# A graph network's edge loop: rings and body of eight groups, loads split evenly over two queues, and the table P in three bf16 parts

## The chip, the cores and the metric

The kernel is one program on one core of a Trainium2 chip. The metric is the device time of the program in microseconds (us); lower is better. The engines are TensorE (PE, with its weight loads as PEld), VectorE (DVE), ScalarE (ACT), GpSimd (POOL) and SyncE (SP). SP, ACT and POOL also issue DMA transfers.

## The reference

Four graph networks run one after the other on 3,125 nodes and 103,125 edges, each followed by a residual and a layer norm. The change touches the second, called L1: node features are 128 wide, and four layers update them along the edges.

```python
for i in range(L):                                      # L = 4
    ef = jnp.concatenate([h[row], h[col], edge_attr], axis=1)
    ef = jax.nn.silu(ef @ edge_w1[i] + edge_b1[i])
    ef = jax.nn.silu(ef @ edge_w2[i] + edge_b2[i])
    ef = ef * edge_mask
    agg = jax.ops.segment_sum(ef, row, num_segments=n)
    nf = jnp.concatenate([h, agg], axis=1)
    nf = jax.nn.silu(nf @ node_w1[i] + node_b1[i])
    nf = nf @ node_w2[i] + node_b2[i]
    h = (h + nf) * node_mask
```

## The kernel before

**Tables.** The first edge product is split: P = h @ W1[0:128] and Q = h @ W1[128:256] are worked out once per node and layer and stored in DRAM as p_tab and q_tab, in 25 blocks of 128 nodes. For each block PE does one product of 256 columns (line 1715), DVE copies it out of PSUM (line 1724), and SP writes its halves (lines 1730, 1731) from two buffers.

**The edge loop.** The edges, sorted on the chip, fill 840 tiles of 128, three tiles to a group, so 280 groups in each layer (`edge_mlp`). For a group:

- `first` (PE) sums into the PSUM area z1, 128 features by 384 edges: the edge attributes (line 1515), for each of the three tiles a block of P times a one-hot matrix that picks each edge's row (line 1517), for the third tile of three groups in four a block of Q picked in the same way (line 1519), and for the other tiles rows of Q that POOL gathered by an indirect DMA (issue at line 1472), turned by a transpose (line 1522);
- `one` (ACT, line 1574) is the first Silu, from z1 to h1;
- `second` (PE, line 1531) multiplies h1 by W2 into z2, which holds the bias beforehand; `two` (ACT, line 1581) is the second Silu, from z2 to h2; `seed` (DVE, line 1607) then puts the bias into z2 for the next group;
- `sums` (PE, line 1542) adds h2 through a weighted one-hot matrix into the PSUM columns of the target nodes. Their addresses are loaded into PE's registers once for two groups (line 963, called from `sums`).

DVE builds the one-hots: `oht` for P (line 1618), `ohn` for Q (line 1617), `ohm` for the sums (line 1626), and hands POOL the indices (line 1602).

**Order.** Every engine works its own program, with semaphores between them. PE's step for group n is first(n), sums(n-2), second(n-1). ACT's is two(n-2), one(n), and for even n its fetch. There is one z1 and one z2, so first(n) waits for one(n-1), and sums(n) and second(n+1) wait for seed(n), which waits for two(n).

**Transfers.** All inputs of a group lie in rings of four slots. For a pair of groups SP issues the row numbers for `oht` (`places`) and `ohn` (`nears`), the edge attributes (`eat`), one or two blocks of Q, and four blocks of P (lines 1495, 1496). ACT issues the other two blocks of P (line 1567), in its own program between one(n) and two(n-1). SP and ACT load the DRAM addresses into registers before (line 963). The pair n, n+1 is fetched once z1 of group n-3 is done.

**The loop.** `turns` writes out two rounds of four groups, then a hardware loop (branch at line 932) whose body is four groups, run 67 times, then a last round.

Of the kernel before, what the change touches and what calls it, by code (L numbers as in the profile page):

```python
# [13 lines left out]
P = 128  # L14
# [6 lines left out]
U = 4  # L21
# [4 lines left out]
M3 = 3  # L26
G3 = NT // M3
K3 = G3 // U
GW = M3 * P
NONE = U - 1  # L30
NA = K3 * NONE
# [23 lines left out]
def gnn_kernel(nc, a, out):  # L55

    with ExitStack() as ctx:
# [51 lines left out]
        p_tab = dram("p_tab", [NP, HID])  # L109
# [817 lines left out]
        def turns(eng, step, rounds=K):  # L927

            for k in (0, 1):
                for h in range(U):  # L930
                    step(k, h)
            with eng.Fori(2, rounds - 1) as k:
                for h in range(U):
                    step(k, h)
            for h in range(U):
                step(rounds - 1, h)
# [494 lines left out]
        m_got = [sem(f"m_got{h}") for h in range(U)]  # L1431
        m_pl, m_sp, m_act = ([sem(f"m_{n}{q}") for q in range(2)] for n in ("pl", "sp", "act"))
        Z1, Z2 = 3584, NP

        def edge_mlp(layer, we36, w2, b1, b2):
# [4 lines left out]
            def here(k, h, lag=0):  # L1440
                return there(k, h, lag, G3)

            def gathered(h):
                return 3 if h == NONE else 2

            with ExitStack() as st:
                qidx = sb(f"qidx{layer}", [P, U, M3], I32, st)
                qg = sb(f"qg{layer}", [P, U, M3, HID], F32, st)
                pb = sb(f"pb{layer}", [P, U, M3, HID], F32, st)
                qb = sb(f"qb{layer}", [P, U, HID], F32, st)  # L1450
                places = sb(f"places{layer}", [P, U, GW], BF16, st)
                nears = sb(f"nears{layer}", [P, U, P], BF16, st)
                eat = sb(f"eat{layer}", [36, U, GW], BF16, st)
                oht = sb(f"oht{layer}", [P, U, GW], F32, st)
                ohn = sb(f"ohn{layer}", [P, U, P], F32, st)
# [5 lines left out]
                with nc.Block() as block:  # L1461
                    @block.gpsimd
                    def _(pool):
                        def gather(k, h):
                            n = k * U + h
                            if here(k, h, U):

                                pool.wait_ge(m_z1, g0 + n - U + 1)
# [5 lines left out]
                        turns(pool, gather, K3)  # L1474

                    @block.sync
                    def _(sp):
                        def fetch(k, h):
                            if h % 2:
                                return  # L1480
                            q, n = h // 2, k * U + h
                            if here(k, h, U):
# [9 lines left out]
                            for i in range(2 - q):  # L1492
# [5 lines left out]
                        turns(sp, fetch, K3)  # L1498

                    @block.tensor  # L1500
                    def _(pe):
# [5 lines left out]
                        def first(k, h):  # L1507

                            n, q = k * U + h, h // 2
                            if here(k, h, 1):  # L1510
                                pe.wait_ge(m_h1, g0 + n)
                            pe.wait_ge(m_sp[q], 16 * (7 - q) * (k0 + k + 1))
                            pe.wait_ge(m_act[q], 32 * (k0 + k + 1))
# [4 lines left out]
                            if h != NONE:  # L1518
# [6 lines left out]
                        def second(k, h):  # L1525

                            n = k * U + h
# [6 lines left out]
                        def sums(k, h):  # L1534

                            n = k * U + h
                            if h % 2 == 0:
                                to[:] = address(mybir.EngineType.PE, to_p[0:1, bass.ds(k * 2 + h // 2, 1), :].rearrange("a g j -> a (g j)"), (NB - 1) * P)
# [6 lines left out]

                        def step(k, h):
                            first(k, h)
# [4 lines left out]
                        turns(pe, step, K3)  # L1552
                        sums(K3 - 1, U - 2)
                        second(K3 - 1, U - 1)
                        sums(K3 - 1, U - 1)

                    @block.scalar
                    def _(act):
                        def fetch(k, h):
                            q, n = h // 2, k * U + h  # L1560
                            if not here(k, h):
                                return
                            if here(k, h, U):
                                act.wait_ge(m_z1, g0 + n - 2)
                            at = address(mybir.EngineType.Activation, at_p[0:1, bass.ds(n + 1, 1), 1:3].rearrange("a g j -> a (g j)"), (NB - 1) * P)
                            for j in range(2):
                                act.dma_start(pb[:, h + 1, 1 + j, :], p_tab[bass.ds(at[j], P), :]).then_inc(m_act[q], 16)

                        def one(k, h):
                            n = k * U + h  # L1570
# [5 lines left out]
                        def two(k, h):  # L1576
                            n = k * U + h
# [5 lines left out]
                        def step(k, h):  # L1583
# [3 lines left out]
                            if h % 2 == 0:  # L1587
                                fetch(*moved(k, h, 2))
                        fetch(0, 0)
                        turns(act, step, K3)  # L1590
                        two(K3 - 1, U - 2)
                        two(K3 - 1, U - 1)

                    @block.vector
                    def _(dve):
                        def indices(k, h):
                            if not here(k, h):
                                return
                            if here(k, h, U):
# [353 lines left out]
```

## Time and profile before

| | |
|---|---|
| median of 3 runs | 8,981.45 us (8,978.94 to 8,988.67) |
| the profiled execution | 9,007.83 us, its span 9,006.1 us |
| mean granted clock of TensorE | 0.792 |
| L1's edge loops, four of them | within 2,367.5 to 6,366 us |
| PE, DVE, ACT, POOL busy | 74%, 56%, 31%, 57% of the span |

The median of the runs is the figure that the change is compared with. The profile comes from another, single execution, somewhat longer than the median, and every duration in the text is from it. Times in the views are counted from the start of its span. A matmul of f32 operands appears as two instructions in the trace, one of bf16 as one.

### The profile page before, as it was taken

To read this page: it belongs to the slowest core of one execution; us is meant where nothing else is said; L and a number is where in the kernel's file an instruction comes from. 1 tells how busy PE (TensorE), PEld (TensorE's weight loads), DVE (VectorE), ACT (ScalarE), POOL (GpSimd) and SP (SyncE) were. 2 spreads that over 40 slices of the span, in tenths; PEclk is the share of its full clock that TensorE was granted. 3 is DMA by queue.
4 is the path that set the end of the run, shared out by engine and by line. 5 is a ranking of instruction groups with operands and counts; after the bars stand their busy time and mean duration, and the time that the engine had idled before them with its cause. 6 is when DMAs were issued, how large, how long until landed. Compare 5 with 4: busy or idle time off the path is not lost. (4 is left out here: it accounts for less than half of the span.)

```text
span 9006.1 us, 230609 instructions
## 1 busy us (share of the span) xinstructions
PE 6678.6 (74%) x51782; PEld 5543.5 (62%) x51783; DVE 5014.9 (56%) x13561; ACT 2799.6 (31%) x8299; POOL 5100.8 (57%) x7138
## 2 busy tenths in 40 slices
PE   1222226767799978999799988999766666888998
PEld 1111114555577757777577767878455555786998
DVE  6333346867355545555455545555322222998999
ACT  1222204544233323333233322333133333222554
POOL 3777736755366636666366645666167776221554
PEclk8555555555799989999899999999655555998999
DMA  2000004433366646666455555666311000332232
GB/s 63 3 3 3 3 29 138 119 100 110 110 166 165 164 112 165 165 166 164 107 164 164 164 121 159 169 166 167 90 31 7 7 7 6 78 82 57 73 72 60
DMA packets 1288626, 877.60 MB, mean 97 GB/s; under 512 B 448518, under 2 KB 1192859, under 8 KB 1287640
## 3 DMA queue, kind: packets, MB, share of 16 engines
q1 hardware_dynamic: 991510, 618.55, 25.3%
q0 software_dynamic: 134272, 178.98, 9.3%
q10 hardware_dynamic: 162752, 78.98, 3.1%
q8 instruction: 41, 0.67, 0.0%
q14 instruction: 51, 0.42, 0.0%
HBM read 832.60 MB, written 50.91 MB: 98 GB/s over the span
## 5 line engine op out<-in xcount | busy, mean ns | idle before, releaser
L1472 POOL DMA_INDIRECT qg<-q_tab,qidx x2520 | 2393.5, 950 | 1444.0 <-DVE qidx L1602 736.5
L1607 DVE COPY ps<-b 128x384 f32<-128x384 f32 x1120 | 628.2, 561 | 1640.7 <-ACT h L1581 1609.1
L1067 PE MATMUL ps<-rhs_i,ohi 128*128 128x128 f32 (+2 forms) x8640 | 1215.1, 266 | 209.8 <-issue 198.0
L1067 PEld LDWEIGHTS ps<-rhs_i,ohi 128*128 128x128 f32 (+1 forms) x8640 | 998.8, 162 | 340.3 <-issue 281.2
L1033 POOL COPY near<-x 128x48 bf16 x2160 | 675.7, 351 | 788.4 <-PE ps L1056 432.9
L1542 PE MATMUL ps<-ohm,h 128*128 128x128 f32 x6720 | 1001.1, 285 | 146.6 <-DVE ps L1607 136.6
L1195 POOL DMA_INDIRECT got_m<-y_tab,idx_m x832 | 815.5, 980 | 474.2 <-issue 251.7
L1517 PE MATMUL ps<-oht,pb 128*128 128x128 f32 x6720 | 1060.5, 295 | 0.0
L1574 ACT ACTIVATE h<-ps,b 128x384 f32<-128x384 f32 x1120 | 650.2, 581 | 1292.6 <-PE ps L1522 1245.2
L1542 PEld LDWEIGHTS ps<-ohm,h 128*128 128x128 f32 x6720 | 842.0, 192 | 281.5 <-issue 275.7
L1581 ACT ACTIVATE h<-ps 128x384 f32<-128x384 f32 x1120 | 549.1, 490 | 1432.5 <-PE ps L1531 1343.5
L375 POOL DMA_INDIRECT list_by_src<-ring,rpos x808 | 783.0, 969 | 348.7 <-issue 255.0
L1212 PE MATMUL ps<-rhs_m,ohi_m 128*128 x2880 | 668.4, 403 | 415.5 <-ACT rhs_m L1238 386.7
L1517 PEld LDWEIGHTS ps<-oht,pb 128*128 128x128 f32 x6720 | 845.2, 193 | 196.9 <-issue 196.9
L1626 DVE TENSOR_SCALAR ohm<-iota_row,loc_p,w_p 128x128 f32<-128x128 f32 x3360 | 961.0, 347 | 0.0
L1531 PE MATMUL ps<-w,h 128*128 128x128 f32 x6720 | 940.2, 276 | 0.0
L1128 DVE TENSOR_TENSOR ohi<-iota_row,dst_i 128x512 f32<-128x512 f32 (+1 forms) x1080 | 929.9, 861 | 0.0
L1212 PEld LDWEIGHTS ps<-rhs_m,ohi_m 128*128 128x128 f32 x2880 | 636.7, 328 | 448.0 <-issue 447.8
L1531 PEld LDWEIGHTS ps<-w,h 128*128 128x128 f32 x6720 | 847.6, 193 | 0.0
L1252 DVE TENSOR_TENSOR ohi_m<-iota_row,dst_i 128x512 f32<-128x512 f32 x360 | 249.2, 693 | 833.5 <-PE ps L1212 829.4
L1123 DVE TENSOR_SCALAR oht_i<-places_i,iota_p 128x512 bf16<-128x512 bf16 (+1 forms) x1080 | 512.5, 475 | 177.6 <-PE ps L1067 160.1
L1031 POOL COPY near<-z 128x384 bf16 x720 | 344.8, 508 | 375.9 <-PE ps L1056 305.0
(438 smaller groups left out, 8629.8 us busy)
## 6 DMA issues: line engine op xcount, KB each, us to landing
pb<-p_tab SPq DMA_DIRECT2D x2240, 64.0 KB
places<-place_by_turn SPq DMA_DIRECT2D x560, 192.0 KB
places_i<-place_by_meeting SPq DMA_DIRECT2D x360, 256.0 KB, 3.4
places_i<-place_by_meeting SPq DMA_DIRECT2D x720, 128.0 KB, 3.1
pb<-p_tab ACTq DMA_DIRECT2D x1120, 64.0 KB
qb<-q_tab SPq DMA_DIRECT2D x840, 64.0 KB
qg<-q_tab,qidx POOLq DMA_INDIRECT x2520
eat<-rows_by_turn SPq DMA_DIRECT2D x560, 54.0 KB
```

The source lines that it names most:

```text
L375: pool.indirect_dma_start(list_s[:, :], IndirectOffsetOnAxis(ap=rpos[:, h, c:c + 1], axis=0), ring[:, h, c, :], None).then_inc(scattered[h ...
L1033: m = pool.tensor_copy(near[:, h, j, :], table[:, bass.ds(at[j], 48)])
L1067: m = pe.matmul(ps[:, bass.ds(to[j], width)], ohi[:, h, j, :], rhs[:, h, j, 0:width], start=False, stop=True, skip_group_check=True)
L1128: dve.tensor_tensor(ohi[:, h, :, :], iota_row[:, None, :].to_broadcast([P, M, P]), dst_i[:, bass.ds(n * M, M)][:, :, None].to_broadcast([P ...
L1195: pool.indirect_dma_start(got[:, h, j, :], None, y_tab, IndirectOffsetOnAxis(ap=idx[:, h, j:j + 1], axis=0)).then_inc(d_got[h], 16)
L1212: m = pe.matmul(ps[:, bass.ds(to[j], 32)], ohi[:, h, j, :], rhs[:, bass.ds(at[j], 1), :].rearrange("p t f -> p (t f)"), start=False, stop= ...
L1472: pool.indirect_dma_start(qg[:, h, j, :], None, q_tab, IndirectOffsetOnAxis(ap=qidx[:, h, j:j + 1], axis=0)).then_inc(m_got[h], 16)
L1517: pe.matmul(z1[:, j * P:(j + 1) * P], pb[:, h, j, :], oht[:, h, j * P:(j + 1) * P], start=False, stop=False)
L1531: m = pe.matmul(z2[:, j * P:(j + 1) * P], h1[:, h % 2, j * P:(j + 1) * P], w2, start=False, stop=True, skip_group_check=True)
L1542: m = pe.matmul(ps[:, bass.ds(to[M3 * (h % 2) + j], P)], h2[:, h % 2, j, :], ohm[:, h % 2, j, :], start=False, stop=True, skip_group_check ...
L1574: act.activation(h1[:, h % 2, :], z1, ACT.Silu, bias=b1).then_inc(m_h1, 1)
L1626: m = dve.tensor_scalar(ohm[:, h % 2, j, :], iota_row[:, :], loc_p[:, bass.ds(t, 1)], w_p[:, bass.ds(t, 1)], ALU.is_equal, ALU.mult)
```

## The change

In L1's edge loop the rings have eight slots and the loop body eight groups (`U3 = 8`), with 32 passes of the hardware loop in a layer. A pair is fetched once z1 of group n-7 is done. SP issues the three P blocks of the even group, ACT those of the odd one, six groups ahead. The two `nears` transfers of a pair become one. The indices are handed to POOL five groups ahead. The register load for `sums` stands ahead of `first` in even steps. P is stored as three bf16 parts (each the rounding of what the parts before leave), 768 bytes a row for 512; `oht` is bf16; each f32 product of line 1517 becomes three bf16 products with the same one-hots. The tables are written through four buffers: ACT rounds P and copies Q out of PSUM, four DVE operations make the other two parts.

```diff
+U3 = 8
-K3 = G3 // U
+K3 = G3 // U3
-        p_tab = dram("p_tab", [NP, HID])
+        p_tab = dram("p_tab", [NP, 3 * HID], BF16)
...
-                pb = sb(f"pb{layer}", [P, U, M3, HID], F32, st)
+                pb = sb(f"pb{layer}", [P, U3, M3, 3 * HID], BF16, st)
-                oht = sb(f"oht{layer}", [P, U, GW], F32, st)
+                oht = sb(f"oht{layer}", [P, U3, GW], BF16, st)
...
                         def fetch(k, h):                                  # SP
-                                sp.wait_ge(m_z1, g0 + n - 2)
+                                sp.wait_ge(m_z1, g0 + n - U3 + 2)
...
-                            for i in range(2 - q):
-                                sp.dma_start(nears[:, h + i, :], near_p[bass.ds((n + i) * M3 + 2, 1), :].to_broadcast([P, P])).then_inc(m_pl[q], 16)
+                            sp.dma_start(nears[:, h:h + 2, :],
+                                         near_p[bass.ds(n * M3, 2 * M3), :].rearrange("(a g j) p -> a g j p", a=1, j=M3)[:, :, 2, :].to_broadcast([P, 2, P])).then_inc(m_pl[q], 16)
...
                             for j in range(M3):
                                 sp.dma_start(pb[:, h, j, :], p_tab[bass.ds(at[j], P), :]).then_inc(m_sp[q], 16)
-                            sp.dma_start(pb[:, h + 1, 0, :], p_tab[bass.ds(at[4], P), :]).then_inc(m_sp[q], 16)
...
                         def first(k, h):                                  # PE
                             for j in range(M3):
-                                pe.matmul(z1[:, j * P:(j + 1) * P], pb[:, h, j, :], oht[:, h, j * P:(j + 1) * P], start=False, stop=False)
+                                for q_ in range(3):
+                                    pe.matmul(z1[:, j * P:(j + 1) * P], pb[:, h, j, q_ * HID:(q_ + 1) * HID], oht[:, h, j * P:(j + 1) * P], start=False, stop=False)
...
-                            if h % 2 == 0:
-                                to[:] = address(mybir.EngineType.PE, to_p[0:1, bass.ds(k * 2 + h // 2, 1), :].rearrange("a g j -> a (g j)"), (NB - 1) * P)
+                        def take(k, h):
+                            to[:] = address(mybir.EngineType.PE, to_p[0:1, bass.ds(k * (U3 // 2) + h // 2, 1), :].rearrange("a g j -> a (g j)"), (NB - 1) * P)
...
                         def step(k, h):
+                            if h % 2 == 0 and here(k, h, 2):
+                                take(*moved(k, h, -2))
                             first(k, h)
...
                         def fetch(k, h):                                  # ACT
-                            at = address(mybir.EngineType.Activation, at_p[0:1, bass.ds(n + 1, 1), 1:3].rearrange("a g j -> a (g j)"), (NB - 1) * P)
-                            for j in range(2):
-                                act.dma_start(pb[:, h + 1, 1 + j, :], p_tab[bass.ds(at[j], P), :]).then_inc(m_act[q], 16)
+                            at = address(mybir.EngineType.Activation, at_p[0:1, bass.ds(n + 1, 1), 0:4].rearrange("a g j -> a (g j)"), (NB - 1) * P)
+                            for j in range(M3):
+                                act.dma_start(pb[:, h + 1, j, :], p_tab[bass.ds(at[j], P), :]).then_inc(m_act[q], 16)
...
                             if h % 2 == 0:
-                                fetch(*moved(k, h, 2))
+                                fetch(*moved(k, h, 6))
...
-                            indices(*moved(k, h, U - 1))
+                            indices(*moved(k, h, 5))
...
+                    @block.scalar                                         # the tables
+                    def _(act):
+                            act.activation(p_out[:, b % 4, 0, :], banks[b % 4][:, 0:HID], ACT.Copy)
+                            act.activation(q_out[:, b % 4, :], banks[b % 4][:, HID:2 * HID], ACT.Copy).then_inc(pq_hi, 1)
...
-                            dve.tensor_copy(pq[:, b % 2, :, :], banks[b % 2][:, 0:2 * HID].rearrange("p (k f) -> p k f", k=2)).then_inc(to_pe.sem, 1)
+                            v_chain(dve, dve.tensor_tensor(r, banks[b % 4][:, 0:HID], p3[:, 0, :], ALU.subtract))
+                            v_chain(dve, dve.tensor_copy(p3[:, 1, :], r))
+                            v_chain(dve, dve.tensor_tensor(r, r, p3[:, 1, :], ALU.subtract))
+                            dve.tensor_copy(p3[:, 2, :], r).then_inc(to_pe.sem, 1)
```

## Rows read from the trace of the kernel before

**Rows 1.** The page: engine totals, DMA queues, DMA issues (last: us to landing).
```profile
PE 6678.6 (74%) x51782; PEld 5543.5 (62%) x51783; DVE 5014.9 (56%) x13561; ACT 2799.6 (31%) x8299; POOL 5100.8 (57%) x7138
...
q8 instruction: 41, 0.67, 0.0%
...
places_i<-place_by_meeting SPq DMA_DIRECT2D x720, 128.0 KB, 3.1
```

**Rows 2.** A window: busy (count) of PE, PEld, DVE, ACT, POOL; clock, DMA, GB/s.
```profile
2700.00:2800.00 100.00, 93.54 (x699) 79.92 (x698) 57.98 (x209) 33.12 (x62) 65.72 (x70) 1.00 0.61 168
```

**Rows 3.** Line 1515: ns min/median/max, first and last start; all layers' idle time.
```profile
L1515 PEld LDWEIGHTS ps<-eat,we x280: 92/92/100, 2367.5 to 3300.1; 36*128 36x128 bf16 x140
...
L1515 PEld LDWEIGHTS ps<-eat,we x280: 92/93/101, 3389.5 to 4319.8; 36*128 36x128 bf16 x140
...
  DMA pb<-p_tab: 203.2, 240
```

**Rows 4.** Timeline of four groups in layer 0: start, us, engine, line.
```profile
3002.07 0.58 ACT L1574 ACTIVATE h<-ps,b 128x384 f32<-128x384 f32 x1 [2.27 <-PE ps L1522]
...
3002.53 0.83 PE L1531 MATMUL ps<-w,h 128*128 128x128 f32 x6
3002.82 0.85 ACTq L1567 DMA_DIRECT2D pb<-p_tab  x2
...
3003.30 0.33 PE L1515 MATMUL ps<-eat,we 36*128 36x384 bf16 x1
...
3003.86 0.49 ACT L1581 ACTIVATE h<-ps 128x384 f32<-128x384 f32 x1 [1.21 <-PE ps L1531]
3004.23 0.30 PEld L1519 LDWEIGHTS ps<-ohn,qb 128*128 128x128 f32 x2
...
3004.38 0.56 DVE L1607 COPY ps<-b 128x384 f32<-128x384 f32 x1 [2.63 <-ACT h L1581]
...
3004.56 0.38 PE L1522 MATMUL ps<-ident,qg 128*128 128x128 f32 x2
...
3005.08 0.93 PE L1542 MATMUL ps<-ohm,h 128*128 128x128 f32 x6
...
3005.84 0.83 PE L1531 MATMUL ps<-w,h 128*128 128x128 f32 x6
...
3006.61 0.33 PE L1515 MATMUL ps<-eat,we 36*128 36x384 bf16 x1
...
3006.77 0.49 ACT L1581 ACTIVATE h<-ps 128x384 f32<-128x384 f32 x1 [1.22 <-PE ps L1531]
...
3009.63 0.33 PE L1515 MATMUL ps<-eat,we 36*128 36x384 bf16 x1
...
3013.03 0.33 PE L1515 MATMUL ps<-eat,we 36*128 36x384 bf16 x1
...
3015.94 0.33 PE L1515 MATMUL ps<-eat,we 36*128 36x384 bf16 x1
```

**Rows 5.** Lines 963, 932 and 1567 by source: ns min/median/max, first and last start.
```profile
L963 PEldq TENSOR_LOAD <-to_p x1: 590/590/590, 3006.1 to 3006.1; - x1
...
L963 PEldq TENSOR_LOAD <-to_p x1: 591/591/591, 3013.2 to 3013.2; - x1
...
L963 ACTq TENSOR_LOAD <-at_p x2: 489/491/493, 3002.2 to 3008.6; - x2
...
L932 PEldq COMPARE_BRANCH  x1: 208/208/208, 3012.0 to 3012.0; - x1
...
L1567 ACTq DMA_DIRECT2D pb<-p_tab x60: 339/350/390, 3002.8 to 3194.2; - x60
```

**Rows 6.** Timeline in the last edge pass: weight loads of a bf16 stream, and the next.
```profile
8502.12 0.68 PEld L1056 LDWEIGHTS ps<-near,oht_i 128*128 128x128 bf16 x12
...
8502.82 0.30 PEld L1067 LDWEIGHTS ps<-rhs_i,ohi 128*128 128x128 f32 x2
```

**Rows 7.** Groups by line while the tables of layer 1 are written (3346 to 3380).
```profile
L1724 DVE COPY pq<-ps 128x256 f32<-128x256 f32 x25 | 10.6, 425 | 32.0 <-DMA q_tab<-pq 18.9 <-PE ps L1715 13.1
```

More of the change, by code:

```diff
@@ L925, in _, with turns @@
                         dve.tensor_copy(to_p[0:1, hs, 0:6], banks[3][0:1, 0:HN].rearrange("a (g j) -> a g j", j=6)).then_inc(c_blk, 1)
-        def turns(eng, step, rounds=K):
+        def turns(eng, step, rounds=K, ring=U):
             for k in (0, 1):
-                for h in range(U):
+                for h in range(ring):
                     step(k, h)
             with eng.Fori(2, rounds - 1) as k:
-                for h in range(U):
+                for h in range(ring):
                     step(k, h)
-            for h in range(U):
+            for h in range(ring):
                 step(rounds - 1, h)
@@ L1430, in gnn_kernel @@
             sem("m_" + n) for n in ("idx", "oht", "ohm", "z1", "h1", "z2", "h2", "sum", "seed"))
-        m_got = [sem(f"m_got{h}") for h in range(U)]
-        m_pl, m_sp, m_act = ([sem(f"m_{n}{q}") for q in range(2)] for n in ("pl", "sp", "act"))
+        m_got = [sem(f"m_got{h}") for h in range(U3)]
+        m_pl, m_sp, m_act = ([sem(f"m_{n}{q}") for q in range(U3 // 2)] for n in ("pl", "sp", "act"))
         Z1, Z2 = 3584, NP
@@ L1440, in here, with blocks, moved @@
             def here(k, h, lag=0):
-                return there(k, h, lag, G3)
+                return not isinstance(k, int) or lag <= k * U3 + h < G3
             def gathered(h):
-                return 3 if h == NONE else 2
-            with ExitStack() as st:
-                qidx = sb(f"qidx{layer}", [P, U, M3], I32, st)
-                qg = sb(f"qg{layer}", [P, U, M3, HID], F32, st)
-                pb = sb(f"pb{layer}", [P, U, M3, HID], F32, st)
[L1450 to L1453, printed above, removed]
-                oht = sb(f"oht{layer}", [P, U, GW], F32, st)
-                ohn = sb(f"ohn{layer}", [P, U, P], F32, st)
+                return 3 if h % 4 == 3 else 2
+            def blocks(q):
+                return 2 - q % 2
+            def moved(k, h, by):
+                d, slot = divmod(h + by, U3)
+                return (k + d if d else k), slot
+            with ExitStack() as st:
+                qidx = sb(f"qidx{layer}", [P, U3, M3], I32, st)
+                qg = sb(f"qg{layer}", [P, U3, M3, HID], F32, st)
+                pb = sb(f"pb{layer}", [P, U3, M3, 3 * HID], BF16, st)
+                qb = sb(f"qb{layer}", [P, U3, HID], F32, st)
+                places = sb(f"places{layer}", [P, U3, GW], BF16, st)
+                nears = sb(f"nears{layer}", [P, U3, P], BF16, st)
+                eat = sb(f"eat{layer}", [36, U3, GW], BF16, st)
+                oht = sb(f"oht{layer}", [P, U3, GW], BF16, st)
+                ohn = sb(f"ohn{layer}", [P, U3, P], F32, st)
                 ohm = sb(f"ohm{layer}", [P, 2, M3, P], F32, st)
@@ L1491, in fetch @@
                             at = address(mybir.EngineType.SP, at_p[0:1, bass.ds(n, 2), :].rearrange("a g j -> a (g j)"), (NB - 1) * P)
-                            for i in range(2 - q):
+                            for i in range(blocks(q)):
                                 sp.dma_start(qb[:, h + i, :], q_tab[bass.ds(at[4 * i + 3], P), :]).then_inc(m_sp[q], 16)
@@ L1551, in step @@
                                 second(*moved(k, h, -1))
[L1552 to L1555, printed above, removed]
+                        turns(pe, step, K3, U3)
+                        take(K3 - 1, U3 - 2)
+                        sums(K3 - 1, U3 - 2)
+                        second(K3 - 1, U3 - 1)
+                        sums(K3 - 1, U3 - 1)
                     @block.scalar
@@ L1587, in step @@
                             if h % 2 == 0:
-                                fetch(*moved(k, h, 2))
[L1589 to L1592, printed above, removed]
+                                fetch(*moved(k, h, 6))
+                        for h in (0, 2, 4):
+                            fetch(0, h)
+                        turns(act, step, K3, U3)
+                        two(K3 - 1, U3 - 2)
+                        two(K3 - 1, U3 - 1)
                     @block.vector
@@ L1633, in step @@
                             build(*moved(k, h, 1))
-                            indices(*moved(k, h, U - 1))
+                            indices(*moved(k, h, 5))
                             if here(k, h, 1):
                                 build_m(*moved(k, h, -1))
-                        for h in range(U - 1):
+                        for h in range(5):
                             indices(0, h)
@@ L1642, in _ @@
                         dve.tensor_copy(z2.rearrange("p (j f) -> p j f", j=M3), b2[:, None, :].to_broadcast([P, M3, HID])).then_inc(m_seed, 1)
-                        turns(dve, step, K3)
-                        seed(K3 - 1, U - 2)
-                        build_m(K3 - 1, U - 1)
-                        seed(K3 - 1, U - 1)
+                        turns(dve, step, K3, U3)
+                        seed(K3 - 1, U3 - 2)
+                        build_m(K3 - 1, U3 - 1)
+                        seed(K3 - 1, U3 - 1)
         with ExitStack() as st:
@@ L1653, in gnn_kernel @@
             wpq = sb("wpq", [P, 2, HID], F32, st)
-            pq = sb("pq", [P, 2, 2, HID], F32, st)
+            q_out = sb("q_out", [P, 4, HID], F32, st)
+            p_out = sb("p_out", [P, 4, 3, HID], BF16, st)
+            left = sb("left", [P, 2, HID], F32, st)
             we = sb("we", [36, HID], F32, st)
@@ L1668, in gnn_kernel @@
             xT = sb("xT1", [FIN, NP], F32, st)
-            pq_out = [sem("pq_out0"), sem("pq_out1")]
-            pq_n = [0, 0]
+            pq_out = [sem(f"pq_out{i}") for i in range(4)]
+            pq_hi = sem("pq_hi")
+            pq_n = [0] * 4
             with nc.Block() as block:
```

84 lines of the change are left out of this document (44 added, 40 removed).

## The prediction

> **What bounds the kernel now.** I read the page first: TensorE is the busiest engine, 74% of the span [rows 1]. The share is a mean over stages, so I went by windows next: in L1's edge loop PE is busy for 93.5 of 100 us at a granted clock of 1.00, which is the 2.4 GHz level, with the DMA engines at 0.61 [rows 2]. The change touches this loop and the stage that writes its tables. The loop runs over 280 groups in each of four layers. The instructions of line 1515, the first matmul of each group, give its length: 932.6 and 930.3 us in the two layers shown [rows 3], so 4 x 931.5 = 3,726 us, 3.33 us for a group. The same view says that PE waited 203.2 us there, in 240 gaps, for a P transfer [rows 3]: nearly once in each pass of the loop (268 passes).
>
> 93% busy could mean that PE sets the pace alone. The timeline of four groups shows that it does so only in every second one [rows 4]. Call n the even group whose first Silu starts at 3002.07. ACT's order is: two(n-2), one(n), the fetch of P blocks, two(n-1). The fetch issues two transfers from 3002.82 to 3003.67, and two(n-1) starts at 3003.86, although second(n-1) was done at 3002.53 + 0.83 = 3003.36. In the other step there is no fetch, and two(n) starts 0.10 after the end of second(n) (3005.84 + 0.83, then 3006.77). So ACT's issuing makes the Silu 0.4 us late, and everything hangs on it: the seed copy on DVE (3004.38 to 3004.94), sums(n-1) at 3005.08, second(n) at 3005.84, first(n+2) at 3006.61 [rows 4]. first(n+1) had ended at 3004.56 + 0.38 = 3004.94, so PE stood waiting. This chain is what the reader is to see: ACT issues DMAs on the path that sets the end. Four groups took 3003.30 to 3015.94, 12.64 us; 280 such fours are 3,539 us, and the 187 us up to 3,726 are the P waits and the four starts.
>
> **The change part by part.**
>
> *Rings of eight.* Now SP issues pair n when group n-3 has released its slot, so SP has some two groups' time for the eight or ten issues of a pair. With eight slots a pair may be fetched some six groups ahead. ACT's fetch too goes for a pair six groups ahead. The P waits should go. 203.2 us hold the four loop starts, which stay (some 5 us each, an estimate), so 183 at most; since 187 us of surplus also hold the slow starts, I take -160 us (bounds -120 and -183).
>
> *Even split.* SP does three P transfers for the even group, ACT three for the odd one: one issue fewer on SP, which is then never last, and one more on ACT, which is on the chain. One issue takes 0.350 us [rows 5], two 0.85 [rows 4], so a third costs 0.50. The register load before them (0.491 us, two values) becomes one of four values; PE's load of six takes 0.590 [rows 5], so 0.025 us a value, +0.05. It begins with one(n) and ends as it does, so this shows in full. Together +0.55 us per pair of groups, bounds 0.50 and 0.60. Behind it on ACT stand two(n-1) and one(n+1), behind these the seed and sums(n-1). The price is nothing only if some cover were there, and the 0.4 us of lateness above say that none is left.
>
> *P in three bf16 parts.* In first(n), the edge-attribute matmul and three f32 products take 3003.30 to 3004.23, 0.93 us [rows 4]. They become one and nine bf16 matmuls with their weight loads. A stream of just this kind, 12 loads and matmuls of 128x128 on 128 columns, stands in the last edge pass: the next kind follows after 8502.82 - 8502.12 = 0.70 us, 0.058 each [rows 6]. Nine are 0.52; the 384-column matmul is 0.17 at that rate, or 0.26 as now if its gap to the next load stays. So 0.69 to 0.78, and first(n) is 0.15 to 0.24 us shorter; I take 0.20. Of two groups only first(n+2) lies on the chain; first(n+1) merely ends sooner and waits longer for the seed. So it counts once per pair.
> The Trainium skill speaks against this part (TensorE: Matmul & The Clock Gate, "Back-to-back issue gap"): it gives about 81 ns for each matmul of 128 columns in a stream of loads and matmuls. By that page nine are 0.73, nothing is saved, and as an estimate the sum below would be some 100 us larger. The trace disagrees with its 0.058, and I go by the trace.
>
> Per pair: 0.55 - 0.20 = +0.35 us, x 560 pairs = +196 us (bounds 560 x 0.26 = 146 and 560 x 0.45 = 252).
>
> *The address load on PE moves ahead of first().* The 0.59 us load of the targets now starts at 3006.1, just behind the issue of first(n+2), which PE takes up at 3006.61 [rows 4, 5]: the sequencer is about half a us ahead, and that covers nearly all of it. 0 to 0.1 us in 432 even steps, I take 0.03: +13. After a branch the lead is gone: the branch takes 0.208 us at 3012.0, first() starts at 3013.03 and the load at 3013.2 [rows 4, 5]. There nearly the whole load comes onto the path, now in the 32 passes of each layer: 0.5 us (0.3 to 0.7) x 128 = +64. Halving the number of passes gives nothing back, since PE's queue covers a branch today (3013.03 follows 3009.63 by 3.40, against 3.31 for the same kind of step).
>
> *More bytes.* A P row grows from 512 to 768 bytes. In 100 us, with 31 groups (62 Silu on ACT), 16.8 MB are moved, 540 KB a group; with 96 KB more it is 1.18 times that, in a longer period: a DMA share near 0.7 [rows 2]. Hidden, as long as the rings are ahead.
>
> *bf16 one-hots, joined nears, indices five ahead.* DVE and POOL only get work off or earlier; DVE has slack before each seed. Nothing.
>
> *The tables.* 25 blocks a layer. Today DVE is busy for 10.6 us in 25 copies, waits 18.9 for the DMA of q_tab and 13.1 for PE, most of that before the first copy [rows 7]: 29.5 to 42.6 us, so 1.2 to 1.7 a block, nearer to the first. Afterwards four DVE operations of 128 columns in a chain follow two on ACT. 256 columns take 0.425; half as wide, between 0.2 and 0.43 each, so 0.8 to 1.7 us a block. I take the present 1.2 and 0 us (bounds -40 and +40 over 100 blocks).
>
> Sum: -160 + 196 + 13 + 64 + 0 = **+113 us**. The profiled execution took 9,007.8 us (span 9,006.1) and should take 9,121. It was 26 us above the median of the runs, 8,981.45; on that the forecast is 9,094, rounded to **9,095 us**. Low bounds together give -183 + 146 + 0 + 38 - 40 = -39, high ones -120 + 252 + 43 + 90 + 40 = +305.
>
> **Rivals.**
> *The third issue is hidden (the other side).* If ACT's extra issue cost nothing, first() were still shorter and the P waits gone: -160 - 112 + 13 + 64 = -195, 8,786 us. For it: ACT is busy for 31% only. Against it: two(n-1) starts right behind the last issue. It decides from an issue cost of 0.35 us: at that, -195 + 560 x 0.35 is zero. 9%.
> *The bf16 products save nothing.* Loads, not columns, could set their pace between f32 neighbours. Then +112: 9,207. Against it is the 0.058; for it, that that stream has one moving tile for three products. 11%.
> *The P waits stay,* because rows of 768 bytes land later or the queues are full: +160, 9,255. 5%.
> *The loop body is too long to stay with the sequencer.* In 100 us PE runs 699 matmuls and 698 loads [rows 2], 186 in a pass of 13.3 us, and a pass of eight groups with the nine products will have 420 (46.5 and 6 more, by eight). The instruction queue brought only 41 packets of 16 KB in the whole span [rows 1], so today's passes run without a reload. If a pass had to wait for one transfer (3.1 us to landing is the nearest row [rows 1]), 128 x 3.1 = 397 more: 9,492. 4%. A rule of the Trainium skill stands behind this (Runtime: NRT & Kernel Launch, "Instruction fetch mechanics"): a taken branch out of the window that is held waits for a fetch, blocks of 256 instructions. No run here shows a loop so long.
>
> **How the numbers follow.** The forecast has 68%, its own range 9,030 to 9,165; 3% stay for what I don't see, the clock among it: PE idles 0.55 + 0.20 = 0.75 us more per pair, and could fall to 1.2 GHz. To leave out no more than 2 in 10, the range goes up through the bf16 rival and down to near the low bounds: 8,985 to 9,220. About 0.2% (18 us) is what a measurement tells from no change. Faster by more: the first rival and a tail of the forecast, 11%. Within: 6%. Slower: 83%.
>
> **What would show it.** In the timeline two(n-1) should start about 1.0 us after second(n-1) ends, in steps with a fetch, and 0.1 in the others; PE should stand still about 0.9 us before each odd sums (0.14 now). No P wait but at the loops' starts. From the first matmul of a group to the load of the Q product 0.73 us for 0.93. After each branch, first() should lag by half a us. Four groups should take 12.64 + 0.7 + about 0.3, 13.6 to 13.7. I am wrong if the issues on ACT become shorter or leave the chain, or if P waits of today also hid time that I count twice.

## The result: faster by 0.7%, where slower was forecast

The changed kernel takes 8,921.13 us (median of 4 runs, 8,908.29 to 8,929.49) against 8,983.93 for the kernel before in the same comparison: a ratio of 0.9929, 95% interval 0.9912 to 0.9946. The forecast was 9,095 us, slower with a chance of 83%, and its range began at 8,985. The profiled execution took 8,926.24 us, its span 8,924.5 us, 81.6 less than the span of before. The mean granted clock is 0.794 (0.792 before).

Where do the 81.6 us lie? The first matmul of each group is now at line 1523. This is the view of that line, first for layer 0, then for layer 1, then the idle time over all four layers. The columns are those of [rows 3]. The view adds up the idle time of PE and of PEld, so one and the same stop can be in it twice.

```profile
L1523 PEld LDWEIGHTS ps<-eat,we x280: 91/93/103, 2364.0 to 3283.1; 36*128 36x128 bf16 x140
...
L1523 PEld LDWEIGHTS ps<-eat,we x280: 91/92/103, 3371.4 to 4279.9; 36*128 36x128 bf16 x140
...
  issue: 111.7, 268
  DMA pb<-p_tab: 49.7, 8
```

The loops of the four layers take 919.1, 908.5, 919.6 and 913.5 us, 3,660.6 together, first group's start to last group's. Before, the same four were 932.6, 930.4, 938.4 and 920.7, 3,722.1 together. So the loops give 61.5 us and everything outside them 20.1. The wait for P went as foreseen, from 203.2 us in 240 gaps [rows 3] to 49.7 in 8: the four starts of a loop, each counted for PEld and for PE. On PE alone it went from 181.2 us in 236 gaps to 23.1 in 4.

The timeline shows what became of ACT's chain [rows 4]. This is one pair of groups of the kernel after, with the step behind the loop's branch at its end. Line 1588 is `one`, 1581 the P issues on ACT, 1595 `two`, 1540 `second`, 1526 the P products, 1622 `seed`, 1549 `sums`.

```profile
3003.44 0.09 PEld L1523 LDWEIGHTS ps<-eat,we 36*128 36x128 bf16 x1
...
3003.71 0.50 PEld L1526 LDWEIGHTS ps<-oht,pb 128*128 128x128 bf16 x9 [0.17 <-issue]
...
3004.17 0.30 PEld L1528 LDWEIGHTS ps<-ohn,qb 128*128 128x128 f32 x2
...
3004.20 0.56 DVE L1622 COPY ps<-b 128x384 f32<-128x384 f32 x1 [1.25 <-ACT h L1595]
...
3004.92 0.58 ACT L1588 ACTIVATE h<-ps,b 128x384 f32<-128x384 f32 x1 [0.75 <-PE ps L1531]
...
3005.01 0.93 PE L1549 MATMUL ps<-ohm,h 128*128 128x128 f32 x6
...
3005.55 1.34 ACTq L1581 DMA_DIRECT2D pb<-p_tab  x3
...
3005.77 0.83 PE L1540 MATMUL ps<-w,h 128*128 128x128 f32 x6
...
3006.99 0.49 ACT L1595 ACTIVATE h<-ps 128x384 f32<-128x384 f32 x1 [1.49 <-PE ps L1540]
...
3008.31 0.93 PE L1549 MATMUL ps<-ohm,h 128*128 128x128 f32 x6 [0.34 <-DVE ps L1622]
...
3015.43 0.75 PEld L1540 LDWEIGHTS ps<-w,h 128*128 128x128 f32 x6
...
3016.72 0.09 PEld L1523 LDWEIGHTS ps<-eat,we 36*128 36x128 bf16 x1 [0.54 <-issue]
```

Three issues take 3005.55 to 3006.89, and `two` follows 0.10 behind, as forecast. But it is only 0.39 us late (`second` ends at 3006.60), not 1.0. This is one of the mildest pairs: over all passes of the hardware loop the median lateness in the steps with a fetch is 0.59 us (0.51 before). Two things keep it below the forecast. The first stands in front of the issues: from the start of `one` to the first issue there are 0.63 us here, and 0.75 before (3002.07 to 3002.82, [rows 4]), where 0.05 more was expected. From `one` to `two` it is 2.07 us against 1.79 in the same pair before, +0.28 where I had +0.55; the medians over all passes, 2.10 and 1.82, say the same. The second is that `second` itself now starts later behind `one`, 0.67 us in the median for 0.47: with `first` shorter, the `sums` in front of it has to wait for its seed in this step too, which the prediction didn't have. (In a_f32 below, with P in f32, it is 0.47 again, and `two` is 0.78 late.) In the pair shown `first` is over at 3004.88, the seed at 3004.76, and `sums` starts at 3005.01. For the first of the two, the view of the register loads says why, here for the kernel after from 3000 to 3032:

```profile
L963 PEldq TENSOR_LOAD <-to_p x5: 589/593/600, 3002.4 to 3028.5; - x5
...
L963 SPq TENSOR_LOAD <-at_p x5: 690/692/705, 3003.1 to 3029.1; - x5
...
L963 ACTq TENSOR_LOAD <-at_p x5: 306/307/310, 3005.1 to 3031.1; - x5
```

ACT loads four values in 0.307 us. Two values took it 0.491 [rows 5]. The longer load is the cheaper one.

### The profile page after: what moved, and what is told of

Its sections match the earlier page's. It is cut to its first block and busy times, and to the rows that moved or that the text cites. A ratio compares the mean times of both kernels' runs of the same rounds, so it can differ in the third digit from the quotient of the medians.

```text
span 8924.5 us, 233638 instructions
## 1 busy us (share of the span) xinstructions
PE 6479.8 (73%) x55142; PEld 5299.9 (59%) x55143; DVE 4955.1 (56%) x13861; ACT 2834.7 (32%) x8499; POOL 5094.9 (57%) x7138
## 5 line engine op out<-in xcount | busy, mean ns | idle before, releaser
L1549 PE MATMUL ps<-ohm,h 128*128 128x128 f32 x6720 | 1034.1, 291 | 380.7 <-DVE ps L1622 371.4
L1526 PE MATMUL ps<-oht,pb 128*128 128x128 bf16 x10080 | 766.2, 222 | 0.0
L1526 PEld LDWEIGHTS ps<-oht,pb 128*128 128x128 bf16 x10080 | 572.3, 98 | 197.1 <-issue 197.1
L1123 DVE TENSOR_SCALAR oht_i<-places_i,iota_p 128x512 bf16<-128x512 bf16 (+1 forms) x1080 | 512.8, 475 | 177.8 <-PE ps L1067 160.2
```

The source lines that it names most:

```text
L1526: pe.matmul(z1[:, j * P:(j + 1) * P], pb[:, h, j, q_ * HID:(q_ + 1) * HID], oht[:, h, j * P:(j + 1) * P], start=False, stop=False)
L1549: m = pe.matmul(ps[:, bass.ds(to[M3 * (h % 2) + j], P)], h2[:, h % 2, j, :], ohm[:, h % 2, j, :], start=False, stop=True, skip_group_check ...
```

## The experiments

Each expectation names the theories that it sets against each other. In the runs on ACT's register load and issues the first of them is that these stand in series with `two`, so that each counts in full. Two terms come back below: *loops* is the sum of the four loops, first group's start to last group's, from each run's trace; the period of slot h is the mean time, over the passes of the hardware loop, up to the first matmul of the group in place h of the body from that of the group before it. So h=0 is the step behind the branch. Where two runs are compared that were not measured side by side, the kernel before, which ran along each time, had medians of 8,977 to 8,984 us.

### The register load alone

**b_four:** the kernel before, with ACT's load of two values made one of four.

```diff
-at = address(mybir.EngineType.Activation, at_p[0:1, bass.ds(n + 1, 1), 1:3].rearrange("a g j -> a (g j)"), (NB - 1) * P)
+at = address(mybir.EngineType.Activation, at_p[0:1, bass.ds(n + 1, 1), 0:4].rearrange("a g j -> a (g j)"), (NB - 1) * P)
...
-    act.dma_start(pb[:, h + 1, 1 + j, :], p_tab[bass.ds(at[j], P), :]).then_inc(m_act[q], 16)
+    act.dma_start(pb[:, h + 1, 1 + j, :], p_tab[bass.ds(at[1 + j], P), :]).then_inc(m_act[q], 16)
```

> The kernel before with one edit: ACT's register load takes four aligned addresses (0:4) and not two (1:3), and uses the middle two. Theory A (the price of ACT's register load was misjudged: four aligned values take 0.309 us in other rows, the pair at an odd offset 0.490, and the load stands on the chain before the transfers' issue): the load falls to 0.31, the second Silu after a fetch starts 0.18 us sooner, 560 x 0.18 = 101 us off, so 8,880. Rival B (a load costs more with more values, as the prediction had it, 0.025 us each): +0.05 x 560, 9,012. Rival C (ACT's issuing isn't on the chain): no change.

8,956.27 us, ratio 0.9981 (0.9971 to 0.999); loops 3,681.5, 40.6 less than before. The direction is that of theory A, the size is a fifth of it. **b_pair0:** two values from the start of the row, so that blocks 0 and 1 go by ACT, block 2 by SP.

```diff
-sp.dma_start(pb[:, h + 1, 0, :], p_tab[bass.ds(at[4], P), :]).then_inc(m_sp[q], 16)
+sp.dma_start(pb[:, h + 1, 2, :], p_tab[bass.ds(at[6], P), :]).then_inc(m_sp[q], 16)
...
-at = address(mybir.EngineType.Activation, at_p[0:1, bass.ds(n + 1, 1), 1:3].rearrange("a g j -> a (g j)"), (NB - 1) * P)
+at = address(mybir.EngineType.Activation, at_p[0:1, bass.ds(n + 1, 1), 0:2].rearrange("a g j -> a (g j)"), (NB - 1) * P)
...
-    act.dma_start(pb[:, h + 1, 1 + j, :], p_tab[bass.ds(at[j], P), :]).then_inc(m_act[q], 16)
+    act.dma_start(pb[:, h + 1, j, :], p_tab[bass.ds(at[j], P), :]).then_inc(m_act[q], 16)
```

> The kernel before, with ACT's pair of addresses taken at the aligned offset (0:2) in place of 1:3; ACT fetches P blocks 0 and 1 of the odd group, SP block 2. Theory A1 (the offset makes the load dear): 0.31 us or less, time as in the run with four values, 8,880. Theory A2 (a count other than four makes it dear): 0.49 us, no change, 8,982.

8,968.28 us, 0.9991 (0.998 to 1.0003): no change that can be told, so theory A2. **a_eight:** the kernel after, with eight values loaded on ACT in place of four.

```diff
-at = address(mybir.EngineType.Activation, at_p[0:1, bass.ds(n + 1, 1), 0:4].rearrange("a g j -> a (g j)"), (NB - 1) * P)
+at = address(mybir.EngineType.Activation, at_p[0:1, bass.ds(n, 2), :].rearrange("a g j -> a (g j)"), (NB - 1) * P)
...
-    act.dma_start(pb[:, h + 1, j, :], p_tab[bass.ds(at[j], P), :]).then_inc(m_act[q], 16)
+    act.dma_start(pb[:, h + 1, j, :], p_tab[bass.ds(at[4 + j], P), :]).then_inc(m_act[q], 16)
```

> The changed kernel with ACT's register load made of eight values, of which it uses the last four. Theory A: the load takes 0.6 to 0.7 us for 0.309 and all of the difference is on the chain: 0.3 to 0.38 x 560 = 168 to 213 us over the changed kernel, 9,090 to 9,135. Rival C (issuing isn't on the chain): 8,921.

9,038.99 us, 1.0067 (1.005 to 1.0084), loops 3,779.1. The load takes 0.55 us and not 0.6 to 0.7, and the loss is smaller accordingly. Here are the loads of b_four, b_pair0 and a_eight, in that order, and under them a line of the kernel before from another stage, where ACT loads four values:

```profile
L963 ACTq TENSOR_LOAD <-at_p x3: 307/308/315, 3002.2 to 3014.8; - x3
```
```profile
L963 ACTq TENSOR_LOAD <-at_p x2: 492/499/506, 3002.6 to 3009.0; - x2
```
```profile
L963 ACTq TENSOR_LOAD <-at_p x3: 549/554/556, 3001.3 to 3014.9; - x3
```
```profile
L949 ACTq TENSOR_LOAD <-from_at x1080: 303/309/528, 1415.6 to 8961.2; - x180
```

So two values cost 0.49 to 0.50 us, from the row's first element or its second, four 0.31, eight 0.55. In the kernel after the 0.25 us from four to eight are worth 118 us of median (0.21 a pair): the load stands on the chain almost in full. With the load at its old price of 0.49 the change would, by my estimate, have lost 0.18 x 560 = 100 us more, and been slower. The last of the four rows is the one I should have looked for: it was in the trace of before, and I scaled two engines' loads to a price instead.

b_four also shows why the same edit brings little in the kernel before. `two` is 0.2 us earlier (period of h=2 3.40 to 3.22 us), but the waits for P grow from 203.2 us in 240 gaps to this:

```profile
  DMA pb<-p_tab: 268.1, 284
```

With four slots SP's transfers are a second chain right behind the first: what ACT gives, the next P wait takes back in part. The run shows the waits; that they are what takes it back is my reading, which the same edit with long rings bears out below.

### The three blocks on ACT

**a_two:** the kernel after, with SP issuing four P blocks and ACT two, as before; ACT's load stays one of four values.

```diff
+    sp.dma_start(pb[:, h + 1, 0, :], p_tab[bass.ds(at[4], P), :]).then_inc(m_sp[q], 16)
...
-    for j in range(M3):
-        act.dma_start(pb[:, h + 1, j, :], p_tab[bass.ds(at[j], P), :]).then_inc(m_act[q], 16)
+    for j in range(2):
+        act.dma_start(pb[:, h + 1, 1 + j, :], p_tab[bass.ds(at[1 + j], P), :]).then_inc(m_act[q], 16)
```

> The changed kernel with the loads split as before: ACT fetches two P blocks of a pair (register load of four kept), SP four. Theory A (ACT's issuing holds the chain): the second Silu after a fetch starts 0.1 us after second() for 0.57, 560 x 0.47 = 263 us off at most, 8,660, if SP with 5.5 us of issuing for a pair of 5.9 keeps up; if SP becomes the bound, P waits come back. Rival (the even split is what removed the P waits): slower than 8,921.

8,692.78 us, 0.9678 (0.9662 to 0.9695), loops 3,422.8: 228 us less than after. P is waited for 51.3 us in 8 gaps, so with long rings the even split had no part in ending those waits. `two` starts here 0.10 us behind `second` in nearly all steps; the median is 0.11 at most in seven slots of the body, 0.35 in the last, before the branch. The timeline of a_two, `second` at line 1541, ACT's issues at 1582, `two` at 1596:

```profile
3002.48 0.85 ACTq L1582 DMA_DIRECT2D pb<-p_tab  x2
...
3002.57 0.83 PE L1541 MATMUL ps<-w,h 128*128 128x128 f32 x6
...
3003.50 0.49 ACT L1596 ACTIVATE h<-ps 128x384 f32<-128x384 f32 x1 [1.07 <-PE ps L1541]
```

The issues end at 3003.33, before `second` does at 3003.40. Two issues fit in the cover, the third sticks out.

**a_spread:** the kernel after, with its three issues on ACT dealt over both steps: the register load and one issue behind `one` of the even step, two behind `one` of the odd step, from registers kept.

```diff
+    kept[:] = at
+    issue(h, part)
+def issue(h, part):
+    for j in part:
+        act.dma_start(pb[:, h + 1, j, :], p_tab[bass.ds(kept[j], P), :]).then_inc(m_act[h // 2], 16)
...
-        fetch(*moved(k, h, 6))
+        fetch(*moved(k, h, 6), (0,))
+    elif here(*moved(k, h, 5)):
+        issue(moved(k, h, 5)[1], (1, 2))
```

> The changed kernel with ACT's three issues spread: register load and one issue after the even first Silu, two issues after the odd one. ACT waits 1.4 us between a first Silu and the next second Silu where there is no fetch, so each part fits. Theory A: both second Silus start 0.1 us after second(), every period is 2.91 us, 560 x 0.47 = 263 us off, 8,660. Rival (the chain has another holder at 3.4): little change.

8,645.75 us, 0.9628 (0.9612 to 0.9644), loops 3,373.3. Nothing is left out, ACT issues just as many transfers: their place alone is worth 275 us. This is its timeline:

```profile
3011.66 0.93 ACTq L1587 DMA_DIRECT2D pb<-p_tab  x2
...
3012.32 0.83 PE L1540 MATMUL ps<-w,h 128*128 128x128 f32 x6
...
3013.25 0.49 ACT L1601 ACTIVATE h<-ps 128x384 f32<-128x384 f32 x1 [1.13 <-PE ps L1540]
...
3015.26 0.37 ACTq L1587 DMA_DIRECT2D pb<-p_tab  x1
3015.34 0.83 PE L1540 MATMUL ps<-w,h 128*128 128x128 f32 x6
...
3016.27 0.49 ACT L1601 ACTIVATE h<-ps 128x384 f32<-128x384 f32 x1 [1.07 <-PE ps L1540]
```

`two` follows `second` by 0.10 in both kinds of step.

### PE's early register load

**a_take_late:** the kernel after, with the load for `sums` behind `first` again.

```diff
+    first(k, h)
     if h % 2 == 0 and here(k, h, 2):
         take(*moved(k, h, -2))
-    first(k, h)
```

> The changed kernel with PE's register load of the target addresses back behind first(), all else kept. Theory A (the early load costs nothing in plain steps and comes onto the path after each branch, where first() starts 3.8 us after the one before it, for 3.4 elsewhere, and pulls the next step along): about 0.5 us in each of 128 passes, 64 us off, 8,855. Rival (what is late after the branch is the branch itself or the code that follows it, not the load): 8,921.

8,878.12 us, 0.988 (0.986 to 0.99): 43 us less than after, loops 3,614.7, 45.9 less. The step behind the branch goes from 3.82 to 3.42 us; of the other slots h=1 goes from 2.71 to 2.85, h=2 from 3.71 to 3.56, the rest stays. In the timeline of after, above, that step's `first` comes 1.29 us behind the load of `second`; in a plain step it is 0.87, with the early load or without. So this part costs where I put it, after the branch, and next to nothing elsewhere. PE's own idle time before the first matmul says so too: 42.0 us in 124 gaps with nothing that it waits for in the kernel after, nearly one for each of the 128 passes. It is less than forecast (0.4 us a pass for 0.5), and the 13 us for plain steps didn't come.

### The rings and the bf16 parts, each alone

**rings_only:** the kernel before, with rings and body of eight, the joined `nears`, and indices five ahead; P in f32, two values and two issues on ACT, PE's load behind `first`.

```diff
+U3 = 8
-K3 = G3 // U
+K3 = G3 // U3
...
-sp.wait_ge(m_z1, g0 + n - 2)
+sp.wait_ge(m_z1, g0 + n - U3 + 2)
```

> The kernel before with only the rings and the body of eight groups (nears joined, indices five ahead): P in f32, ACT's two blocks by a register load of two, PE's load behind first(). Theory A: the P waits go (203 us, of which some 50 stay at the loops' starts) and nothing else moves: 153 us off, 8,825, so faster than the whole change. Rival (the P waits hide something else that is late at the same place): half of it or less.

8,831.92 us, 0.9835 (0.9819 to 0.9852), loops 3,548.7, 173.4 less than before; P waits 50.6 us in 9 gaps.

**rings_load4:** the same with ACT's load of four values.

```diff
-at = address(mybir.EngineType.Activation, at_p[0:1, bass.ds(n + 1, 1), 1:3].rearrange("a g j -> a (g j)"), (NB - 1) * P)
+at = address(mybir.EngineType.Activation, at_p[0:1, bass.ds(n + 1, 1), 0:4].rearrange("a g j -> a (g j)"), (NB - 1) * P)
...
-    act.dma_start(pb[:, h + 1, 1 + j, :], p_tab[bass.ds(at[j], P), :]).then_inc(m_act[q], 16)
+    act.dma_start(pb[:, h + 1, 1 + j, :], p_tab[bass.ds(at[1 + j], P), :]).then_inc(m_act[q], 16)
```

> The run with rings and body alone, and ACT's register load of four values for two. With the fetches far ahead nothing takes the 0.18 us back: theory A and S, 560 x 0.18 = 101 us off 8,832, 8,731. If the load had been hidden in part, less.

8,715.82 us, 0.9704 (0.968 to 0.9729), loops 3,433.2. With the rings long, the edit that gave 20 us in the kernel before gives 116: 0.206 us a pair in the loops for 0.18 on the load.

**a_f32:** the kernel after with P in f32, its one-hots and its table stage as before.

```diff
-    for q_ in range(3):
-        pe.matmul(z1[...], pb[:, h, j, q_ * HID:(q_ + 1) * HID], oht[...], start=False, stop=False)
+    pe.matmul(z1[...], pb[:, h, j, :], oht[...], start=False, stop=False)
```

> The changed kernel with P as f32 again (table, its writing, one-hots and products as before), rings of eight, even split and the early address load kept. The prediction's term of 0.20 us for each pair holds: first() 0.93 us to the Q load for 0.73, 560 x 0.20 = 112 us more, 9,033. Rival (the bf16 products save nothing on the chain): 8,921.

9,034.2 us, 1.0066 (1.0049 to 1.0083), loops 3,752.4: without the bf16 parts the change is slower than the kernel before. They bring 113 us of median; the spans of the two profiled executions have 91.8 in the loops and 15 outside them. Outside the loops the seven kernels of this text with P in f32 have 5,270.3 to 5,284.0 us, the seven with the parts 5,260.6 to 5,269.2, so the difference stands clear of the scatter, 14 us in the mean. It is the table stage, which was to be level. For layer 1 of the kernel after, the last operation on each of the 25 blocks starts from 3332.5 to 3359.4, 26.9 us, and before from 3347.4 to 3378.2, 30.8; over the four layers it is 105.6 for 124.2. Grouped by line, the four DVE operations are longer together than the one copy of [rows 7], but the copies waited for DMA, and these wait only for ACT, 13.2 us in all with the wait for the first block:

```profile
L1752 DVE TENSOR_TENSOR left<-left,p_out 128x128 f32<-128x128 f32 x25 | 7.5, 301 | 0.9
L1750 DVE TENSOR_TENSOR left<-ps,p_out 128x128 f32<-128x128 f32 x25 | 7.1, 284 | 13.2 <-ACT q_out L1743 13.2
...
L1753 DVE CAST p_out<-left 128x128 bf16<-128x128 f32 x25 | 6.0, 240 | 0.9
L1751 DVE CAST p_out<-left 128x128 bf16<-128x128 f32 x25 | 5.7, 227 | 0.9
```

**bf16_only:** the kernel before with P in three bf16 parts and the new table stage, its rings of four kept.

```diff
-pb = sb(f"pb{layer}", [P, U, M3, HID], F32, st)
+pb = sb(f"pb{layer}", [P, U, M3, 3 * HID], BF16, st)
```

> The kernel before with only P in three bf16 parts (table, its writing, one-hots, nine products), rings and body of four, split four to two. The prediction would have 560 x 0.20 = 112 us off, 8,869. Theory S (in the kernel before a second chain holds the pass of four groups: slot released, SP's issues, landing; what the first chain gives, the P waits take back, as in the run with a load of four on ACT, where 40 of 101 us came out of the loops): P waits grow from 203 to about 260 us, and 30 to 50 us come off, 8,935.

9,132.41 us, 1.0163 (1.0135 to 1.0191). This is a miss, and the largest of the series: a gain was expected, and the same part that brings 113 us in the kernel after costs 150 here. Loops 3,882.3, 160.2 more than before. The waits before the first matmul show where; this is the view of PE alone, where a stop counts once:

```profile
  DMA pb<-p_tab: 361.6, 236
  DVE oht L1619: 88.1, 53
```

Before, they were 181.2 us in 236 gaps and 3.5 in 2. So the P waits are 180.4 us longer in the same number of gaps. One of them in the timeline of bf16_only, from SP's four issues for a pair to the group that waits for them:

```profile
3012.87 1.36 SPq L1495 DMA_DIRECT2D pb<-p_tab  x3
...
3014.42 0.33 SPq L1496 DMA_DIRECT2D pb<-p_tab  x1
...
3018.22 0.33 PE L1515 MATMUL ps<-eat,we 36*128 36x384 bf16 x1 [1.31 <-DMA pb<-p_tab]
```

3.47 us lie between the end of the fourth issue (3014.75) and the matmul. In the 228 steps that wait for P, behind the first two rounds of each layer, the median of this distance is 3.31 to 3.38 us by layer, and 2.43 to 2.49 in the kernel before (231 steps). A block of 96 KB instead of 64 lands some 0.9 us later under this load, and with four slots nothing covers it. The period of h=0 rises from 3.95 to 4.72; in sum the steps up to a group of slot 0 take 197.7 us more, those up to slot 1, where the shorter products show, 38.1 less, the other two are level within 3. The waits put down to `oht` fall in the same steps; whether the row numbers too land later, or DVE is only behind, stays open.

### The best of the parts together

**best:** a_spread with PE's load behind `first`.

> The changed kernel with ACT's issues spread over both steps and PE's register load behind first(). The first gave 275 us, the second 43. Theory: both add, 8,646 - 43, about 8,605. Rival (with ACT off the chain PE's lead over the branch is smaller or larger, so that the load counts otherwise): 8,570 to 8,646.

8,607.13 us, 0.9585 (0.9561 to 0.9609), loops 3,345.3: 4.2% faster than the kernel before, and 314 us below the kernel after. **spread_f32:** the same with P in f32.

> The same with P in f32. Theory A (the bf16 parts paid 0.20 us a pair only because first() stood in ACT's chain; with ACT free, a group takes 2.91 us by the chain of second Silu, seed, sums, second, and f32 lets PE do it in 2.91 too): within 30 us of the run with bf16, 8,605 to 8,635. Rival (bf16 pays per group wherever PE is busy): 0.20 x 1,120 = 224 us more, 8,830.

8,620.17 us, 0.9598 (0.9567 to 0.9629), loops 3,344.2. The loops are equal to 1.1 us; the 13 us between the two lie outside them, in the table stage. The timeline of best shows why shorter products no longer help. `second` is line 1540, `two` 1601, `seed` 1630, `sums` 1549:

```profile
2907.06 0.83 PE L1540 MATMUL ps<-w,h 128*128 128x128 f32 x6
...
2907.99 0.49 ACT L1601 ACTIVATE h<-ps 128x384 f32<-128x384 f32 x1 [1.20 <-PE ps L1540]
...
2908.52 0.56 DVE L1630 COPY ps<-b 128x384 f32<-128x384 f32 x1 [1.04 <-ACT h L1601]
...
2909.32 0.74 PEld L1549 LDWEIGHTS ps<-ohm,h 128*128 128x128 f32 x6 [0.29 <-issue]
...
2910.09 0.83 PE L1540 MATMUL ps<-w,h 128*128 128x128 f32 x6
```

From one `second` to the next, 3.03 us, the chain runs `second`, `two`, `seed`, `sums`, with no wait longer than 0.24 in it, and `first` is not on it. The weight loads stand still for 0.29 us before `sums`, for the seed. With f32 products this room is filled with work, and the group takes as long. How much room the matmuls themselves have left is hard to tell, since their ends are modelled: from 3600 to 3700 us PE is busy for 99.16 us in best and for 100 in spread_f32. That the chain is the limit of best is read from this timeline; no run shortens it.

## Why the prediction was wrong

**The step that failed** is in "Even split": "The register load before them (0.491 us, two values) becomes one of four values; PE's load of six takes 0.590 [rows 5], so 0.025 us a value, +0.05." It is a difference of -0.18 us, not of +0.05: the price doesn't grow steadily with the number of values, and it was scaled between two engines. On the chain it decides the sign of the whole: with -0.18 x 560 = -101 us in place of +28 the same sum is -16.

The loops' 61.5 us can be split by the runs, each step by the loops of two kernels that differ in one part. The order is before, rings_only, rings_load4, (no run), a_f32, after:

| part | predicted, us | loops measured, us | from |
|---|---|---|---|
| rings of eight | -160 | -173.4 | 3,722.1 to 3,548.7 |
| ACT's load, two values to four | +28 (0.05 x 560) | -115.5 | 3,548.7 to 3,433.2 |
| the third issue on ACT | +280 (0.50 x 560) | +273.3 | what is left: 3,752.4 - 45.9 - 3,433.2 |
| PE's early load | +77 (13 + 64) | +45.9 | a_take_late against after |
| P in bf16 | -112 (0.20 x 560) | -91.8 | 3,752.4 to 3,660.6 |
| sum | +113 | -61.5 | |

Of the 174.5 us between the two sums the load is 143.5, the early load 31, the rings 13, the third issue 7, and the bf16 term was 20 too hopeful. The third issue is the one row without a pair of runs of its own, so its agreement with the forecast is weaker than it looks: a_two against after gives 237.8 us for it on the bf16 side. The sizes also hang on the order: in the kernel before, the load of four is worth 40.6 us of the loops (b_four) and not 115.5. Outside the loops 20.1 us came where 0 was taken; some 15 are the tables, inside their bounds.

The signs that were to show the forecast came out smaller in the same way. Four groups take 13.28 us here (3003.44 to 3016.72) for the 13.6 to 13.7 expected, and PE stands still for 0.34 us before the odd `sums` for 0.9.

**What held.** The chain through ACT: `two` directly behind the last issue in every step with a fetch, and a third issue at 0.49 us. The rival, "the third issue is hidden", gave the right sign by the wrong mechanism. The P waits: 153.5 us of the view's sum are gone, 158.1 on PE alone, for 160. The bf16 products: from the first weight load of a group to that of the Q product 0.73 us for 0.93 [rows 4], the nine loads in 0.50. The Trainium skill's figure of about 81 ns a matmul (TensorE: Matmul & The Clock Gate, "Back-to-back issue gap") would make the nine 0.73; in the trace the load of the Q product follows the first of the nine after 0.46 us (3003.71 to 3004.17), 0.051 each, so it disagrees, and a_f32 bears the trace out. The table stage and the bytes: DMA share 0.74 at 201 GB/s, as this window of the kernel after has it, for 0.61 and 168 [rows 2].

```profile
2700.00:2800.00 100.00, 88.89 (x791) 73.24 (x789) 54.42 (x206) 32.91 (x62) 66.31 (x70) 1.00 0.74 201
```

The clock stayed at 1.00 in this window, the 2.4 GHz level, though PE's busy share fell by 4.7 points.

**The loop body.** The rival that a body of eight groups would be fetched anew in each pass is wrong. The page of the kernel after has

```profile
q8 instruction: 57, 0.93, 0.0%
q14 instruction: 70, 0.57, 0.0%
```

The first row has 16 packets more than before [rows 1], the second, which the prediction left out, 19 more (51 before), for 128 passes of the hardware loop. So the body is not brought in anew for each pass. The rule of the Trainium skill that I had put behind that rival (Runtime: NRT & Kernel Launch, "Instruction fetch mechanics") didn't show itself at this length, 483 instructions of PE in a pass of the trace. The same section gives PE room for 2,048, so by the page too the rival had little ground.

**What was not in the prediction.** I took the bf16 term and the rings as independent. bf16_only shows that they are not: alone, the larger blocks cost more in P waits than the products save. In the change the rings go with them, and so the sum could still be made term by term, in that order. The lateness of `second` itself, told with the result, was not in it either.

## What to carry to other kernels

Before an instruction's price is scaled from a neighbour, look through the whole trace for the same instruction with as many values on the same engine: here 1,080 of them stood in another stage. Where an engine both computes on the critical chain and issues transfers, deal its issues over the steps so that each lot ends before the engine's next operand is ready; here that was worth 275 us with no transfer less. And a part that makes transfers larger is to be tried with the ring that covers them: the same bf16 parts cost 150 us with four slots, bring 113 with eight, and 13 once another chain sets the pace.

## What the runs showed of the hardware

- A load of registers on ACT takes 0.49 us for two values, whether they begin at the row's first or second element, 0.31 for four, and 0.55 for eight. PE takes 0.59 for six, SP 0.69 for eight. Why two are dearer than four no run here tells.
- An issue of a P block costs ACT 0.34 us and some 0.15 of register work around it, whether it is 64 or 96 KB (medians 0.345 before, 0.344 in bf16_only). What the bytes lengthen is the way from the issue to the waiting matmul, by some 0.9 us in bf16_only.
